# Block-sparse attention and mixture of experts: keys and values in separate tables, transfers in another order

## What is computed

```python
qb = q.reshape(B, H, M, BS, HD).mean(axis=3)          # M = 8 blocks of BS = 64 tokens
kb = k.reshape(B, H, M, BS, HD).mean(axis=3)
c = jnp.einsum('bhmd,bhnd->bhmn', qb, kb) * SCALE
k_keep = max(1, int(round(M * (1.0 - SPARSITY))))      # 1
thresh = jax.lax.top_k(c, k_keep)[0][..., -1:]
block_mask = (c >= thresh) | jnp.eye(M, dtype=bool)
...
h = jax.nn.gelu(jnp.einsum('nd,edh->enh', xf, w1) + b1[:, None, :], approximate=False)
y = jnp.einsum('enh,ehd->end', h, w2) + b2[:, None, :]
out = jnp.einsum('nk,nkd->nd', gates, y_sel - c_sel + c_sum[None, None, :])
```

## Time and profile before

| | us |
|---|---|
| median of 3 runs | 893.54 |
| lowest, highest | 892.5, 895.87 |
| the profiled execution | 900.17 |
| its span in the trace | 898.5 |

### The profile page before, as it was taken

The page is one execution under the profiler, slowest core; times in us unless marked ns, Lnnn a source line. Parts: engine busy times, 40 slices in busy tenths (PEclk is TensorE's granted clock), DMA queues, the critical chain, the costliest instruction groups (busy, mean ns, idle before and its releaser), DMA issues.

```text
span 898.5 us, 23529 instructions
## 1 busy us (share of the span) xinstructions
PE 827.9 (92%) x9382; PEld 558.8 (62%) x9382; DVE 517.5 (58%) x1526; ACT 460.9 (51%) x754; POOL 174.8 (19%) x176
## 2 busy tenths in 40 slices
PE   3287889999999999999999999999999999999995
PEld 2165667666666666676666567676666666666662
DVE  6073465746575665747566565757566666646321
ACT  2042247374655556374746457374646556473740
POOL 5300011210313031221213021221213031211111
PEclk8598599999999999999999999999999999999998
DMA  8987078676958668685957578675848676771110
GB/s 257 231 213 172 5 215 182 165 178 185 214 155 210 167 184 195 187 193 164 212 159 193 151 199 194 191 191 158 213 145 215 164 204 160 210 159 35 60 59 13
DMA packets 207440, 151.77 MB, mean 169 GB/s; under 512 B 123208, under 2 KB 189648, under 8 KB 203232
## 3 DMA queue, kind: packets, MB, share of 16 engines
q1 hardware_dynamic: 205024, 133.46, 59.8%
q0 software_dynamic: 2304, 16.78, 5.0%
HBM read 95.02 MB, written 50.99 MB: 163 GB/s over the span
## 4 chain that ended last, share of the span: by engine, by line
PE 61%; DMA 20%; ACT 8%; issue 5%; DVE 3%; SPq 2%; POOL 0%; POOLq 0%; ACTq 0%; DVEq 0%
PE y_ps L406 15%; DMA selected<-kv_table,index 8%; PE o_ps L349 6%; PE s_ps L310 5%; DMA kv_chosen<-selected 4%; PE s_ps L338 4%; PE s_ps L264 4%; ACT hid L960 4%; PE s_ps L266 4%; PE s_ps L265 4%; DMA kv_table<-stage 3%; PE o_ps L356 3%; PE a_ps L379 2%; PE v_ps L329 2%; DMA keys<-kv_chosen 2%
## 5 line engine op out<-in xcount | busy, mean ns | idle before, releaser
L406 PE MATMUL y_ps<-hid,w2s 128*128 128x512 f32 x480 | 236.1, 602 | 0.0
L657 DVE TRANSPOSE_TENSOR_REDUCE rmax<-s_ps 128x16 bf16<-128x512 f32 x256 | 168.2, 699 | 70.5 <-PE s_ps L310 70.4
L924 ACT ACTIVATE prob<-s_ps 128x1024 f32<-128x1024 f32 x128 | 131.1, 1024 | 150.6 <-PE s_ps L338 150.5
L960 ACT ACTIVATE hid<-s_ps,b1s 128x512 f32<-128x512 f32 x256 | 171.2, 688 | 38.8 <-PE s_ps L266 35.2
L1050 POOL TENSOR_TENSOR yT<-yT,gate_cols 128x512 f32<-128x512 f32 x48 | 61.4, 1279 | 294.7 <-DVE gate_cols L753 294.2
L310 PE MATMUL s_ps<-qdiag,keys 128*128 128x256 f32 x512 | 95.3, 309 | 24.8 <-DMA keys<-kv_chosen 24.7
L264 PE MATMUL s_ps<-xnhi,w1hi 128*128 128x512 f32 x256 | 113.1, 442 | 1.4
L406 PEld LDWEIGHTS y_ps<-hid,w2s 128*128 128x128 f32 x480 | 83.2, 193 | 43.8 <-issue 40.0
L917 ACT COPY vaug<-v_ps 128x128 f32<-128x128 f32 x128 | 33.9, 265 | 147.4 <-PE v_ps L322 147.3
L666 DVE TENSOR_REDUCE nmax<-v_ps 128x64 bf16<-128x256 bf16 x128 | 54.2, 423 | 95.4 <-PE v_ps L329 95.4
L266 PE MATMUL s_ps<-xnhi,w1lo 128*128 128x512 f32 x256 | 101.4, 396 | 0.0
(11 more groups left out here) (143 smaller groups left out, 1051.5 us busy)
## 6 DMA issues: line engine op xcount, KB each, us to landing
qdiag<-q_table SPq DMA_DIRECT2D x128, 128.0 KB, 3.9
kv_chosen<-selected SPq DMA_DIRECT2D x32, 512.0 KB, 5.5
keys<-kv_chosen SPq DMA_DIRECT2D x32, 512.0 KB, 5.4
gate_cols<-gates SPq DMA_DIRECT2D x64, 256.0 KB, 4.2
kv_table<-stage SPq DMA_DIRECT2D x16, 768.0 KB, 3.9
q_table<-qpair SPq DMA_DIRECT2D x16, 512.0 KB, 3.0
xs<-in_x SPq DMA_DIRECT2D x16, 256.0 KB, 5.7
kv_table<-stage SPq DMA_DIRECT2D x16, 256.0 KB, 2.9
```

The source lines that it names most:

```text
L406: ins = pe.matmul(dst[:], w2s[:, n, :], hid[:, n, :], start=(c == 0), stop=(c == C - 1))
L657: v.tensor_reduce(rmax[m % 2][:, :, half * P // 2:half * P // 2 + HH].rearrange("p k h -> p h k"), s_ps[m % 2][:, half * N:(half + 1) * N] ...
L924: act.activation(prob[m % 2][:].rearrange("p h s -> p (h s)"), s_ps[m % 2][:], ACT.Exp, scale=SCALE).then_inc(exped, 1)
L960: act.activation(hid[:, k, :], up_ps[up_bank(k)], ACT.Gelu, bias=b1s[:, k:k + 1]).then_inc(gelued, 1)
```

## The change

- The table of a batch is split: `k_table` with three planes, `v_table` with one. `KP` is 96, the rows of keys and queries in a score product. The fourth query plane, its zeros and the waits for them go.
- Keys are gathered and passed on by themselves (`sel_k`, 128 rows of 6 KB), values after them (`sel_v`, 128 rows of 2 KB), each with its own semaphores.
- For b >= 1 the stages are q 3, k 2, v 5, products 4 instead of 2, 3, 4, 5. VectorE's choice `a_select` moves from block 5 to block 4, GpSimd's gather from block 6 to block 5, with the gather of values in block 6. ScalarE now makes the high part of the queries (`a_q_high`) from batch 2 on, VectorE only the low part and the sum.
- The gating of the second expert (`c_gated(b - 2, 1)`) moves on VectorE from the end of block 3 to block 4.
- `w2` and `w1` are loaded by a list `heavy` of their own, right after the second batch of `x`; `proj_b` moves to `second`.
- SyncE's transfers stand in another order, and own keys are read in two halves.

```diff
-PLANES = 4
-ROW = PLANES * BS
+PLANES = 3
+KP = HQ * HD * PLANES
...
-            return (2, 0, 1, 3) if b == 0 else (2, 3, 4, 5)
+            return (2, 0, 1, 3) if b == 0 else (3, 2, 5, 4)
...
+            def a_q_low(b):
+                v.wait_ge(q_high, b - 1)
+                total = step(v.tensor_reduce(qsum[:], block_ap(a_ps[:]), AXX, ALU.add))
+                v.tensor_tensor(qlo, a_ps[:], qhi.bitcast(F32), ALU.subtract).then_inc(bank_a.free, 1)
+                return total
...
+                    if b >= 2 and m == 4:
+                        c_gated(b - 2, 1)
...
-                    if ahead and m == 5:
+                    if ahead and m == 4:
                         tied = a_select(b + 1)
...
+            def a_select_values(b):
+                j = b % 2
+                g.wait_ge(index_done, b + 1)
+                g.wait_ge(table_v_out, 16 * (b + 1))
+                if b >= 1:
+                    g.wait_ge(sel_v_out, 16 * b)
+                g.indirect_dma_start(
+                    out=sel_v[:], out_offset=None, in_=table_v[b][:, :],
+                    in_offset=bass.IndirectOffsetOnAxis(ap=index[j][:, 0:1], axis=0)).then_inc(gathered_v, 16)
...
-                        if m == stages(b)[3] + 1:
+                        if m == (4 if b == 0 else 5):
                             a_select(b + 1)
+                        if m == (4 if b == 0 else 6):
+                            a_select_values(b + 1)
...
             load_x(0)
             load(first, weights_in)
             load_x(1)
+            load(heavy, heavy_in)
             s.wait_ge(dve_set, HONE_ZERO)
             load(second, attention_in)
-            s.wait_ge(null_set, 1)
-            for q_rows in qtab:
-                s.dma_start(q_rows.rearrange("(p t) c -> p t c", t=PLANES)[:, 3, :],
-                            prob[0][:, 0:HH, :].rearrange("p h s -> p (h s)")).then_inc(q_null, 16)
             load(third, experts_in)
-            put_high(0)
-            put_low(0, bank_y, bank_v)
+            put_k(0, bank_y)
             put_q(0)
-            take_own(0)
+            take_own(0, 0)
             place_q(0, 0)
-            put_selected(0)
-            take_selected(0)
+            put_v(0, bank_v)
+            put_keys(0, 0)
+            put_keys(0, 1)
+            take_keys(0, 0)
+            put_values(0)
+            take_own(0, 1)
+            take_values(0)
+            take_keys(0, 1)
             place_q(0, 1)
```

More of the change, by code:

```diff
@@ L109, in layer @@
         qhi, qlo = qpair[:, 0, :], qpair[:, 1, :]
-        qdiag = [sb(f"qdiag{i}", [P, QUADS, HQ, N // 2], F32R) for i in range(2)]
-        stage = sb("stage", [P, M, PLANES - 1, BS], F32R)
-        keys = [sb(f"keys{i}", [P, M, QUADS, KEYS], F32R) for i in range(2)]
+        qdiag = [sb(f"qdiag{i}", [KP, QUADS, HQ, N // 2], F32R) for i in range(2)]
+        stage = sb("stage", [P, M, 3, BS], F32R)
+        keys = [sb(f"keys{i}", [KP, M, QUADS, KEYS], F32R) for i in range(2)]
         vals = [sb(f"vals{i}", [P, M, KEYS]) for i in range(2)]
@@ L169, in layer, with per_batch @@
         gm = hid[:, 10, :]
-        table = [nc.dram_tensor(f"kv_table{b}", [H * M, HD * ROW], F32, kind="Internal").ap() for b in range(B)]
-        chosen = [nc.dram_tensor(f"kv_chosen{b}", [H * M, HD * ROW], F32, kind="Internal").ap() for b in range(B)]
+        def per_batch(name, width):
+            return [nc.dram_tensor(f"{name}{b}", [H * M, width], F32, kind="Internal").ap() for b in range(B)]
+        table_k, chosen_k = (per_batch(n, HD * PLANES * BS) for n in ("k_table", "k_chosen"))
+        table_v, chosen_v = (per_batch(n, HD * BS) for n in ("v_table", "v_chosen"))
         gates = [nc.dram_tensor(f"gates{b}", [E * T, P], F32, kind="Internal").ap() for b in range(B)]
@@ L299, in scores @@
                     pe.wait_ge(q_placed[m // HALF], PLACED * (b + 1))
-                if m == 0:
-                    pe.wait_ge(own_k_in[j], 16 * times(b, 2))
                 if m % HALF == 0:
+                    pe.wait_ge(own_k_in[j][m // HALF], 16 * times(b, 2))
                     pe.wait_ge(sel_k_in[j][m // HALF], 16 * times(b, 2))
@@ L849, in vector @@
                         c_gates(b - 1, ranked)
-                    if b >= 2 and m % 2:
+                    if b >= 2 and m in (1, 5, 7):
                         c_gated(b - 2, m // 2)
@@ L979, in scalar @@
                         a_k_high(b + 1)
+                    if b >= 1 and b + 1 < B and m == stages(b)[0]:
+                        a_q_high(b + 1)
                     if b >= 1 and b + 1 < B and m == stages(b)[2]:
@@ L1144, in place_q, with put_keys @@
                                 ).then_inc(q_placed[half], 16)
-            def put_selected(b):
-                s.wait_ge(gathered, 16 * (b + 1))
-                for half in range(2):
-                    r = slice(half * P // 2, (half + 1) * P // 2)
-                    s.dma_start(chosen[b][r, :], selected[r, :]).then_inc(sel_out[half], 16)
+            def put_keys(b, half):
+                r = slice(half * P // 2, (half + 1) * P // 2)
+                s.wait_ge(gathered_k, 16 * (b + 1))
+                s.dma_start(chosen_k[b][r, :], sel_k[r, :]).then_inc(sel_k_out[half], 16)
             def take_keys(b, half):
-                s.wait_ge(sel_out[half], 16 * (b + 1))
+                s.wait_ge(sel_k_out[half], 16 * (b + 1))
                 if b >= 2:
@@ L1220, in sync @@
                 if b + 1 < B:
-                    if b >= 1:
-                        put_q(b + 1)
-                    put_high(b + 1)
-                    if b >= 1:
-                        place_q(b + 1, 0)
-                    put_low(b + 1, bank_a, bank_a)
-                    if b == 0:
-                        put_q(b + 1)
-                    take_own(b + 1)
-                    if b == 0:
-                        place_q(b + 1, 0)
-                    put_selected(b + 1)
-                    take_selected(b + 1)
+                    put_k(b + 1, bank_a)
+                    if b == 0:
+                        put_v(b + 1, bank_a)
+                    for half in range(2):
+                        take_own(b + 1, half)
+                    put_q(b + 1)
+                    place_q(b + 1, 0)
+                    if b >= 1:
+                        put_v(b + 1, bank_a)
+                    for half in range(2):
+                        put_keys(b + 1, half)
+                    for half in range(2):
+                        take_keys(b + 1, half)
+                    put_values(b + 1)
+                    take_values(b + 1)
                     place_q(b + 1, 1)
```

101 lines of the change are left out of this document (52 added, 49 removed).

## The result

| | before | after |
|---|---|---|
| median | 892.6 (20 runs, 888.11 to 899.19) | 903.48 (20 runs, 897.21 to 910.62) |
| the profiled execution | 900.17 | 909.42 |
| its span | 898.5 | 907.6 |

The ratio is 1.0114 [1.0089, 1.0138]. I had forecast 876.5 us, with a range of 866 to 887 us and 0.07 for slower. Sign and size were wrong.

What follows compares the result with a forecast made beforehand. TensorE was taken to bound the steady batches, transfers showing only as delays. Gains of 10.0 (steady), 4.8 (start) and 2.4 us (batch 0 to 1), 17.2 us off the 893.54 us median, gave about 876.5 us, range 866 to 887 us.

Steps and rivals of the forecast that it cites:

- slower: Rival: the value gather holds GpSimd and the value transposes in every batch; 905 us, chance 0.07.
- The step that failed: Steady batches, GpSimd: sum and split queue behind the value gather, 1 to 2 us later, both used after block 7.
- the bound from above: Steady batches, values: a gather as slow as the 1 MB one, 10.28 us, landing values at 297.5 us, 2 us late.
- The keys: Steady batches: key gather issued 3.5 us earlier and taking 6.8 us; keys asked for 6.9 us earlier.
- The steady part: The 13 steady batches: delays of 10.5 us go, less 0.5 us on the engines, a gain of 10.0 us.
- values that keep the delays: Rival: TensorE waits for values about as often as for keys, only start and first step gain; 886 us, chance 0.16.
- The start: Program start: scores at 34.4 us, 7.8 us earlier, but values at 38.5 us limit the gain to 4.8 us.
- The term in the sum: Program start, values: table write at about 24.5 us plus four legs of 3.5 us, values at 38.5 us, gaining 4.8 us.
- the place of the weights: Program start: weights loaded at 3 us let the table be written before the index is ready, 2.7 us.
- Batch 0 to 1: Step from batch 0 to batch 1: keys come over 4 us earlier, so 2.4 us of 2.56 us waiting go.
- the bound of 0: Step from batch 0 to batch 1: the lower bound of the gain, if the values are late.
- The clock: Rival: a shorter gap before batch 1 keeps 2.4 GHz, giving 8 us or more in all; 868 us, chance 0.12.

Runs made afterwards that it cites:

- e1_pool_order: Changed kernel with GpSimd issuing the value gather behind the third expert's sum and the split for `c_up`: 887.75 us, ratio 0.9889.
- e5_weights_old_place: `e1_pool_order` with the expert weight loads back inside the third group of loads, ahead of the table writes: 882.4 us, ratio 0.9857.
- e9_old_place_filler: Changed kernel with value gather behind the split, weights inside the third load group, and 12 filler products behind batch 0's last output projection: 883.45 us, ratio 0.9871.
- e3_heavy_first: Kernel before, with only the two expert weight loads moved to right behind the second block of `x`: 896.82 us, ratio 1.0049.
- the first edit alone: The same run as `e1_pool_order`: changed kernel with the value gather behind the sum and split on GpSimd, 887.75 us.
- the late beginning of batch 1: `e9_old_place_filler` with batch 1's first scores and values behind batch 0's last output projection, batch 2's statistics earlier on VectorE: 878.49 us, ratio 0.9822.
- e7_boundary_filler: `e1_pool_order` with 12 filler products on TensorE behind the last output projection of batch 0: 881.04 us, ratio 0.9854.

## Why the prediction was wrong

**The step that failed** is the one on GpSimd: that behind the value gather the sum of the third expert and the split for `c_up` queue "1 to 2 us later than before; both are used after block 7", costed at nothing. The delay was 3.9 us, and I had named the use but not read the margin to it. Both rows were in the trace of before, and give 2.3 us. The prediction asked what is queued behind the waiting instruction and who waits for that, and then left the price out. Had I subtracted, with my own issue of the table at 274.3 us and landing at 278.6 us, and with the 3.5 us that gather, sum and split take on GpSimd, the split would have ended at 282.1 us, 1.2 us inside the margin; with the 7.2 us that pass in the changed kernel between the table's issue and the gather (226.73 to 233.96 us) it ends at 285.0 us, 1.7 us late. So the price of that one leg decided, and the bound from above (10.28 us), which I used for the value arrival, I did not carry to this queue.

What it cost: 15.9 us over the 13 batches (659.80 - 643.91), 10.0 us of it the waits themselves in 12 times. The other 6 us is time in which TensorE counts as busy (645.05 against 639.09 us): 3.6 us in the two batches in which the clock fell, and 0.2 us in each of the others, for which no run shows a cause. Window of the changed kernel right behind such a wait:

```profile
237.53:240.93 3.40, 3.40 (x11) 2.74 (x12) 2.51 (x13) 1.36 (x2) 1.89 (x3) 0.53 1.16 193
```

**The keys: right.** The gather is issued 23.2 us into the batch, before 26.9 us: 3.7 us earlier, forecast 3.5 us. From its issue to the next transfer it takes 5.2 to 6.9 us, forecast 6.8 us by proportion, before 9.1 us in the batch read (8.8 to 11.4 us over all). The Trainium skill's page "DMA: Bandwidth & Descriptors", section "Anatomy of one DMA", puts a DMA issued by GpSimd at some 2.0 us fixed plus its bytes over 436 GB/s; a quarter of 1 MB less then saves 0.6 us, and taken off the 9.1 us that is an estimate of 8.5 us. The trace does not agree with it, though the own keys were moved from beside the gather too, so that size isn't the only difference. (I had used the figure for SyncE's legs too, which that section does not treat.) SyncE's legs saved less than a quarter:

```profile
k_chosen<-sel_k SPq DMA_DIRECT2D x32, 384.0 KB, 5.0
keys<-k_chosen SPq DMA_DIRECT2D x32, 384.0 KB, 5.2
...
q_table<-qpair SPq DMA_DIRECT2D x16, 512.0 KB, 4.8
```

Before, the first two were 5.5 us and 5.4 us at 512 KB; and `q_table`, of equal size, went from 3.0 us to 4.8 us. It now follows the reads of the own keys in the queue; whether that or the form of its rows is the cause was not tested.

**The steady part: right, once the queue is mended.** `e1_pool_order` takes 643.91 us for 13 batches; the prediction had 654.05 - 10.0 = 644.05 us. TensorE waits for values in none of these, and VectorE in block 4 costs nothing that shows. On the values there was luck in it: I had them land some 43.2 us into the batch (291.5 - 248.3), 4 us ahead of their use. In `e1_pool_order` their last transfer is only issued at 41.0 to 43.1 us, with a median of 3.6 us to landing, against a use at 47.1 us, so that the margin left is an estimated 0.4 to 2.5 us. The matrix products over 96 rows take what those over 128 took (mean 311 ns, before 309 ns), as assumed. Of the rivals, values that keep the delays did not come true; "slower" did in its first half (the value gather holds GpSimd), and by another victim than the value transposes that I put there.

**The start: mis-sized.** Forecast 34.4 us for scores and 38.5 us for values, a gain of 4.8 us. The changed kernel has 36.82 us and 41.58 us: 1.8 us gained at the values (before 43.34 us). The term in the sum is that of the values, and its legs were priced too low: the value table is written at 23.69 us, 0.8 us earlier than I had it, but the four legs take 17.9 us (to 41.58 us), where I had put 14. On the keys' side the index is ready at 19.3 us and the gather waits to 20.31 us for a table that the weights ahead of it hold back by an issue of 3.48 us. I had taken 2.7 us from the place of the weights. The gather goes out 1.3 us earlier than before, but with the weights in their old place it goes out at 19.82 us and 19.86 us (`e5_weights_old_place`, `e9_old_place_filler`), so this edit gave nothing; which other part of the change gives the 1.3 us was not tested. The same edit on the kernel before does not help either (`e3_heavy_first`).

**Batch 0 to 1: wrong.** Forecast 2.4 us gained, by keys. The keys do come in time, but the values don't: 2.1 us of waiting for them in the changed kernel, in place of 2.56 us for both, near the bound of 0 that I had named. SyncE issues the write of the chosen values at 71.42 us, right behind the reads of the keys, and their last leg at 77.14 us. What weighs more is that batch 1 then ran at the low clock for longer, 0.71 over its span against 0.80: from the first values to batch 2 it is 5.1 us more than before. The clock was a rival of mine with the opposite sign. That its stretch varies is seen in the figures above (0.57 and 0.79 in two profiles with the old order, 0.51 to 0.79 in those of the changed kernels without filler); so in the 5.1 us of this one pair of profiles chance has a share that is not known. That a filler at this place shortens the stretch is borne out for the changed kernel, by runs and traces together; for the kernel before it is not.

In the pair of profiles, then, 9.1 us of span are lost: 1.8 us gained up to the first values, 5.1 us lost from there to batch 2, and 5.8 us lost in the 13 steady batches, where I had forecast gains of 4.8, 2.4 and 10.0 us.

Set against the sum: forecast -17.2 us; the first edit alone gives -4.8 us at the median, with the filler -11.8 us (892.84 us before in that set), and with the late beginning of batch 1 -17.4 us (895.88 us before). That the last figure meets the forecast is chance: neither the filler nor the late beginning was in it.

## What to carry to other kernels

When an instruction that waits for a DMA is put into an engine's program, compute the margin of everything behind it, use minus end from the trace of before, and take the upper end of the transfer's price, not the middle; here a margin of 2.3 us met a delay of 3.9 us. Put the waiting instruction behind the work that others wait for: the gather went out at the same time and nothing was lost. A chain with less DMA in it, and no wait on a transfer, isn't yet a faster kernel: where "issue" is the releaser of a matrix product, as before L270 here, read the queues of the other engines too. And where transfers are taken apart, look at the one that goes second; it inherits each delay of the first.

## What the runs showed that I had not expected

- The issue right behind the 1 MB load of `w2s` is long in these profiles: 3.48 us and 3.66 us for the second 1 MB load when both stand at 3 to 4 us (4.07 us in `e7_boundary_filler`), 1.98 us for it at 7.87 us (`e5_weights_old_place`), 1.99 us for a load of 2 KB (before). Most other issues of these loads take 0.3 to 0.5 us, the one behind the second 1 MB load 0.5 to 1.0 us.
- The time of a gather does not follow its bytes: 1 MB 9.2 us, 768 KB 5.8 us, 256 KB still 5.0 us (medians of the pages).
- The new layout moves less (138.67 MB, before 151.77 MB) in more packets (239,408, before 207,440), of which 172,840 are under 512 bytes, before 123,208. What the smaller packets cost was not measured.
- TensorE's clock was at 0.53 over the 3.40 us of the window above, right behind a wait of 1.55 us in the midst of a stretch otherwise at 1.00, and not behind one of 1.90 us in the batch from 403.80 us.
